# Two products over 64 contraction rows in plain float32, in pairs on the halves of the array, in an attention and mixture-of-experts kernel

## The reference, cut to what matters

```
spikes_enc = sigmoid(inputs_embeds @ W_enc + b_enc)          # 128 -> 256
cont = flat @ W_s2c + b_s2c                                  # 256 -> M = 64
probs = softmax(cont @ Wr + br)                              # 64 -> 8 experts
topk_w, topk_idx = top_k(probs, 2)                           # gates of the two best experts
h = relu(einsum('tm,emh->eth', cont, W1) + b1)               # 64 -> 128 for each of 8 experts
y = einsum('eth,ehm->etm', h, W2) + b2                       # 128 -> 64 for each expert
expert_out = einsum('etm,te->tm', y, gate)
spikes_moe = sigmoid(expert_out @ W_c2s + b_c2s)             # 64 -> 256
decoded = spikes_moe @ W_dec + b_dec                         # 256 -> 128
return layernorm(decoded, ln_g, ln_b)
```

## Time and profile before

| what | value |
|---|---|
| time, median of 3 runs | 162.12 us (161.94 to 162.26) |
| profiled execution, first to last instruction (its span; its own time is not listed apart from the runs) | 160.3 us |
| PE matmul busy, share of the span | 138.7 us, 87% |
| DVE busy | 130.0 us, 81% |
| ACT busy | 66.8 us, 42% |
| POOL busy | 29.9 us, 19% |
| granted PE clock | full until the last slices, then half of it |
| shares of the chain of waits that ended last | DVE 55%, PE 23%, issue 9% |

### The profile page before, as it was taken

One profiled execution on the slowest core, in us unless ns is written; L12 is line 12 of the kernel. 1 busy time (PEld: TensorE's weight loads), 2 busy tenths in 40 slices (PEclk: granted clock), 3 DMA queues, 4 the chain that ended last, 5 costly groups with the idle time before them and its releaser, 6 DMA issues.

```text
span 160.3 us, 2496 instructions
## 1 busy us (share of the span) xinstructions
PE 138.7 (87%) x820; PEld 104.4 (65%) x828; DVE 130.0 (81%) x504; ACT 66.8 (42%) x128; POOL 29.9 (19%) x55
## 2 busy tenths in 40 slices
PE   7697999589999989999999799999998889994810
PEld 2254686356589775768897757687994477983700
DVE  1686379999979996699999962897999759979883
ACT  3114662182961317467811246397203566003200
POOL 1452243102013100122211100204310002200131
PEclk9999999999999999999999999999999999999555
DMA  3499300000000000000010000000000010000101
GB/s 97 114 203 222 105 4 2 0 0 0 0 4 0 0 2 0 2 4 0 0 65 4 2 0 0 0 0 4 0 0 0 2 70 0 0 0 0 65 0 65
DMA packets 5597, 4.16 MB, mean 26 GB/s; under 512 B 1987, under 2 KB 4562, under 8 KB 5586
## 3 DMA queue, kind: packets, MB, share of 16 engines
q1 hardware_dynamic: 5586, 4.02, 9.3%
HBM read 2.97 MB, written 1.05 MB: 25 GB/s over the span
## 4 chain that ended last, share of the span: by engine, by line
DVE 55%; PE 23%; issue 9%; POOL 3%; SPq 2%; DMA 2%; ACT 2%; POOLq 1%; DVEq 0%
DVE stats L887 10%; DVE gated L1012 6%; DVE mean_var L890 4%; DVE moe L1022 4%; PE ps_f L718 4%; POOL rstd L352 3%; DVE neg_max L928 3%; DVE attn L903 3%; PE ps_f L638 3%; DVE hn L903 3%; PE ps_f L630 2%; PE ps_s L586 2%; DMA x_in<-in_L_attn_x 2%; DVE x_mid L945 2%; DVE z L1061 2%
## 5 line engine op out<-in xcount | busy, mean ns | idle before, releaser
L352 POOL TENSOR_TENSOR rstd<-var_eps,minus_half 128x2 f32<-128x2 f32 (+1 forms) x32 | 26.1, 815 | 122.9 <-DVE var_eps L896 104.1
L688 PEld LDWEIGHTS ps_f<-w,hidden 128*128 128x128 f32 x256 | 31.0, 192 | 1.8 <-issue 1.3
L688 PE MATMUL ps_f<-w,hidden 128*128 128x64 f32 x256 | 30.3, 272 | 0.5
L443 ACT ACTIVATE hidden<-ps_f,bias_cols 128x512 f32<-128x512 f32 x28 | 18.0, 689 | 9.2 <-PE ps_f L669 9.2
L1022 DVE TENSOR_REDUCE moe<-gated 128x64 f32<-128x512 f32 x16 | 16.6, 1035 | 0.1
L586 PE MATMUL ps_s<-kT,qT 128*128 128x512 f32 x32 | 16.3, 602 | 0.2 <-DVE kT L1092 0.2
L404 ACT ACTIVATE probs<-ps_s,neg_max 128x512 f32<-128x512 f32 x16 | 11.0, 685 | 8.3 <-DVE neg_max L928 8.3
L668 PE MATMUL ps_f<-cont_parts,w_hi 128*128 128x512 f32 x28 | 13.8, 493 | 0.3 <-DVE products L962 0.3
L928 DVE TENSOR_REDUCE neg_max<-ps_s 128x1 f32<-128x512 f32 x16 | 10.8, 685 | 2.9 <-PE ps_s L586 2.8
L409 ACT ACTIVATE probsT<-ps_t 128x512 f32<-128x512 f32 x16 | 9.6, 598 | 7.0 <-PE ps_t L596 7.0
L669 PE MATMUL ps_f<-cont_parts,w_lo 128*128 128x512 f32 x28 | 11.1, 395 | 0.0
(11 more groups left out here) (188 smaller groups left out, 250.8 us busy)
## 6 DMA issues: line engine op xcount, KB each, us to landing
x_in<-in_L_attn_x SPq DMA_DIRECT2D x4, 256.0 KB, 3.8
out<-x_out SPq DMA_DIRECT2D x3, 256.0 KB, 2.0
...
```

The lines of the kernel that those rows point to most:

```text
L352: nc.gpsimd.tensor_tensor(rstd[part], var_eps[part], minus_half[:, t0:t1], ALU.pow).then_inc(g_rstd[n], 1)
L443: nc.scalar.activation(hidden[:, e], hidden_bank(b, e)[:, :], ACT.Relu, bias=bias_cols[:, R_B1 + e:R_B1 + e + 1]).then_inc(a_h, 1)
L688: mm = nc.tensor.matmul(y[:, e * M:(e + 1) * M], hidden[:, e, t * P:(t + 1) * P], w2[:, e], start=False, stop=(e == E - 1))
```

## The change

The operands stay whole and plain float32. `cont` and `moeT` hold the same values in rows 0 to 63 and in rows 64 to 127 (ACT writes them as before, since the weights ahead of them stand twice), and a matmul takes 64 rows of both operands. Of a pair, the one with even number takes rows 0 to 63 and the odd one rows 64 to 127. The splits on DVE, and the waits for them, are gone: PE waits for ACT's `a_hi` and `a_mhi`. The order of PE's stream changes so that hidden units come in pairs. The orders of ACT, POOL and SP stay; DVE's only loses rows.

```
-    def hidden_units(b, e):
-        if e == 0:
-            pe.wait_ge(v_cont, b + 1)
-            if b == 0:
-                pe.wait_ge(v_w1, 2)
-        if e == 1 and 1 <= b < B - 1:
-            pe.wait_ge(v_z1, T * b)
-        if e == 2 and b < B - 1:
-            pe.wait_ge(v_prod, b + 1)
-        if e >= 3:
-            pe.wait_ge(a_h, E * b + e - 2)
-        bank = hidden_bank(b, e)
-        nc.tensor.matmul(bank[:, :], w1_hi[:, e], cont_parts[:, b % 2], start=True, stop=False)
-        nc.tensor.matmul(bank[:, :], w1_lo[:, e], cont_parts[:, b % 2], start=False,
-                         stop=True).then_inc(pe_h, 1)
+    def hidden_pair(b, e):
+        if e == 0:
+            pe.wait_ge(a_hi, b + 1)
+            if b == 0:
+                pe.wait_ge(d_w1, 32)
+            elif b < B - 1:
+                pe.wait_ge(v_z1, T * b)
+        for row in range(2):
+            if e + row == 2 and b < B - 1:
+                pe.wait_ge(v_logit, b + 1)
+            if e + row >= 3:
+                pe.wait_ge(a_h, E * b + e + row - 2)
+            half = slice(row * M, (row + 1) * M)
+            nc.tensor.matmul(hidden_bank(b, e + row)[:, :], w1[half, e + row], cont[half, b % 2],
+                             start=True, stop=True).then_inc(pe_h, 1)
...
-        mm = nc.tensor.matmul(logit_bank(b)[:, 2 * t * E:2 * (t + 1) * E],
-                              cont_parts[:, b % 2, t * P:(t + 1) * P],
-                              w_r[:, :, :].rearrange("p a e -> p (a e)"), start=True, stop=True)
+        mm = nc.tensor.matmul(logit_bank(b)[:, t * E:(t + 1) * E],
+                              cont[0:M, b % 2, t * P:(t + 1) * P], w_r[0:M, :], start=True, stop=True)
...
-    nc.tensor.matmul(slot(F_C2S[c])[:, :], w_c2s_hi[:, c * P:(c + 1) * P], moe_parts[:, b % 2],
-                     start=True, stop=False)
-    nc.tensor.matmul(slot(F_C2S[c])[:, :], w_c2s_lo[:, c * P:(c + 1) * P], moe_parts[:, b % 2],
-                     start=False, stop=True).then_inc(pe_c2s, 1)
+    for c in range(HC):
+        half = slice(c * M, (c + 1) * M)
+        nc.tensor.matmul(slot(F_C2S[c])[:, :], w_c2s[half, c * P:(c + 1) * P], moeT[half, b % 2],
+                         start=True, stop=True).then_inc(pe_c2s, 1)
...
         if more:
-            hidden_units(b, 0)
+            hidden_pair(b, 0)
         if first:
             turn_probs(n, 0)
             scores(n, 2)
-        if more:
-            hidden_units(b, 1)
-            hidden_units(b, 2)
+        hidden_pair(b, 2)
         if first:
             attend(n, 0)
             turn_probs(n, 1)
-        hidden_units(b, 3)
-        hidden_units(b, 4)
+            scores(n, 3)
+        hidden_pair(b, 4)
         if first:
-            scores(n, 3)
             attend(n, 1)
             turn_probs(n, 2)
-        hidden_units(b, 5)
-        hidden_units(b, 6)
-        if more:
             attend(n, 2)
             turn_probs(n, 3)
-        hidden_units(b, 7)
+        if b == 0:
+            attend(n, 2)
+            turn_probs(n, 3)
+        hidden_pair(b, 6)
...
             route(n)
-            for e in range(3):
-                hidden_units(n, e)
+            hidden_pair(n, 0)
             decode(b)
```

More of the change, by code:

```diff
@@ L116, in attention_moe_block @@
         spikes = sb("spikes", [P, 2, HC, S])
-        cont_parts = sb("cont_parts", [P, 2, S], F32R)
-        products = sb("products", [P, 2, T, E])
+        cont = sb("cont", [P, 2, S])
         logits = sb("logits", [P, 2, T, E])
@@ L132, in attention_moe_block @@
         moe = sb("moe", [P, 2, T, 2, M])
-        moe_parts = sb("moe_parts", [P, 2, S], F32R)
+        moeT = sb("moeT", [P, 2, S])
         spikes2 = sb("spikes2", [P, 2, HC, S])
@@ L315, in _ @@
             for half in range(2):
-                sp.dma_start(w1_raw[half * M:(half + 1) * M], W1.rearrange("e m h -> m e h")).then_inc(d_w1, 16)
+                sp.dma_start(w1[half * M:(half + 1) * M], W1.rearrange("e m h -> m e h")).then_inc(d_w1, 16)
             sp.dma_start(w_enc[:, :], W_enc).then_inc(d_enc, 16)
             for half in range(2):
-                sp.dma_start(w_r_raw[half * M:(half + 1) * M], Wr).then_inc(d_router, 16)
+                sp.dma_start(w_r[half * M:(half + 1) * M], Wr).then_inc(d_router, 16)
             sp.dma_start(br_all[:, :], br.partition_broadcast(P)).then_inc(d_router, 16)
@@ L325, in _ @@
             for half in range(2):
-                sp.dma_start(w_c2s_raw[half * M:(half + 1) * M], W_c2s).then_inc(d_c2s, 16)
+                sp.dma_start(w_c2s[half * M:(half + 1) * M], W_c2s).then_inc(d_c2s, 16)
             sp.dma_start(x_in[:, 2], x_dram[2]).then_inc(d_x[2], 16)
@@ L426, in cont_out @@
                     act.wait_ge(v_bcont, 1)
-                nc.scalar.activation(cont_parts[:, b % 2], slot(F_CONT)[:, :], ACT.Identity,
+                nc.scalar.activation(cont[:, b % 2], slot(F_CONT)[:, :], ACT.Identity,
                                      bias=b_cont[:, :]).then_inc(a_hi, 1)
@@ L432, in moe_out @@
                 act.wait_ge(pe_moeT, b + 1)
-                nc.scalar.activation(moe_parts[:, b % 2], slot(F_MT)[:, :], ACT.Identity).then_inc(a_mhi, 1)
+                nc.scalar.activation(moeT[:, b % 2], slot(F_MT)[:, :], ACT.Identity).then_inc(a_mhi, 1)
             def second_exp(b):
@@ L697, in turn_moe, with to_spikes @@
                 mm.then_inc(pe_moeT, 1)
-            def to_spikes(b, c):
-                pe.wait_ge(v_mparts, b + 1)
+            def to_spikes(b):
+                pe.wait_ge(a_mhi, b + 1)
                 if b + 1 < B:
@@ L728, in turn_last_moe, with last_to_spikes @@
                 mm.then_inc(pe_moeT, 1)
-            def last_to_spikes(c, h):
+            def last_to_spikes(h):
                 t0, t1 = LAST[h]
                 part = slice(t0 * P, t1 * P)
-                pe.wait_ge(v_mparts, B + h)
-                for weights, start in ((w_c2s_hi, True), (w_c2s_lo, False)):
-                    mm = nc.tensor.matmul(last_c2s[h][c][:, part], weights[:, c * P:(c + 1) * P],
-                                          moe_parts[:, (B - 1) % 2, part], start=start, stop=not start)
-                mm.then_inc(pe_c2s, 1)
+                pe.wait_ge(a_mhi, B + h)
+                for c in range(HC):
+                    half = slice(c * M, (c + 1) * M)
+                    nc.tensor.matmul(last_c2s[h][c][:, part], w_c2s[half, c * P:(c + 1) * P],
+                                     moeT[half, (B - 1) % 2, part], start=True, stop=True).then_inc(pe_c2s, 1)
             def decode_last(h):
@@ L857, in _ @@
                     to_cont(n)
-                for c in range(HC):
-                    to_spikes(b, c)
+                to_spikes(b)
                 if more2:
@@ L871, in _ @@
             expert_out(B - 1, T - 1)
-            for c in range(HC):
-                last_to_spikes(c, 0)
+            last_to_spikes(0)
             turn_last_moe(1)
             decode_last(0)
-            for c in range(HC):
-                last_to_spikes(c, 1)
+            last_to_spikes(1)
             decode_last(1)
@@ L961, in router_top @@
                 dve.wait_ge(pe_logit, b + 1)
-                nc.vector.tensor_reduce(products[:, i], logit_bank(b)[:, 0:2 * T * E].rearrange(
-                    "p (t a e) -> p t e a", t=T, a=2), AX_X, ALU.add).then_inc(v_prod, 1)
-                dve.wait_ge(v_prod, b + 1)
-                nc.vector.tensor_tensor(logits[:, i], products[:, i], br_all[:, :].unsqueeze(1).to_broadcast([P, T, E]),
+                dve.wait_ge(d_router, 48)
+                nc.vector.tensor_tensor(logits[:, i], logit_bank(b)[:, 0:T * E].rearrange("p (t e) -> p t e", t=T),
+                                        br_all[:, :].unsqueeze(1).to_broadcast([P, T, E]),
                                         ALU.add).then_inc(v_logit, 1)
@@ L1211, in _ @@
                     z_unit(b - 1, 0)
-                if more:
-                    split_moe(b)
                 if more and not more2:
@@ L1221, in _ @@
                     x_norm(m + 1)
-                if more:
-                    split_cont(n)
             z_unit(B - 2, 0)
-            split_last_moe(1)
             z_add(B - 2, 0)
```

58 lines of the change are left out of this document (7 added, 51 removed).

## The result

| what | before | with the change |
|---|---|---|
| time, median | 162.19 us (161.94 to 162.49, 4 runs) | 172.61 us (171.72 to 173.71, 4 runs) |
| ratio | | 1.064, 95% interval 1.0576 to 1.0705 |
| span of the profiled execution | 160.3 us | 169.7 us |
| PE matmul busy | 138.7 us, 87% | 148.7 us, 88% |
| DVE busy | 130.0 us, 81% | 120.8 us, 71% |

The change makes the kernel 6.4% slower, by 10.4 us; the forecast was 170.8 us and the range 165.3 to 177.8. The four runs lie on two levels, 171.7 at a mean granted clock of 0.960 and 173.5 to 173.7 at 0.943; the profiled one is on the lower, and its span is 9.4 above that of before, where 8.7 was forecast.

The account below looks back on a forecast made before the run. Neither DVE nor PE alone was taken to bound the kernel; the chain changes sides. 0.2 + 2.8 + 3.1 + 0.5 + 2.55 - 0.65 + 0.2 = +8.7 on 162.1 gave 170.8 us, range 165.3 to 177.8.

Parts of the forecast that it names:

- pass 0: First pass, order kept but for the pairing: fourth pair +0.3 at expert_out, slack leaves +0.2 (from -0.8 to +1.5).
- `to_spikes`, twice: Product with W_c2s in passes 0 and 1, 1.28 where it took 1.04: +0.5 (from -0.4 to +1.3).
- pass 1: First pair waits for v_z1 with turn_probs and scores queued behind; ACT's copy uncovered; DVE's gates later by +2.8.
- pass 2: Begins like pass 1, with attend(3, 3) ahead of expert_out and turn 3's copy ahead of relu 6: +3.1.
- pass 2 to 3: Unit 2 stands behind decode(2), so second_exp, gates and dec_stats wait: statistics at 135.7, not 133.14, +2.55.
- the end: Last sequence: -0.65 left of DVE's saved 1.40, +0.2 for last_to_spikes(1) in float32 at the low clock.
- price of a pair: Two hidden units on two halves take 1.28 by in-order starts (bounds 0.85 and 1.70), 0.96 before.
- side by side: Rival: a pair's records interleave on the two halves, pair 0.85, queue waits remain: +3.9, time 166.0; chance 0.20.
- switching between half and whole rows: On PE, taken as costing nothing; upper bound 0.20 at each of some 20 switches, +4.
- drains: Rival: changing tiling mode drains the engine, +8.7 and up to 4 more, 174.8 at the most; chance 0.12.
- relief of DVE: Last sequence: the 1.40 us for ACT's copy and split before DVE's gates goes; some -0.65 is left.
- rival of the earlier clock: Rival: PE idles some 2.6 us ahead of turn_last_moe(0), clock falls, expert_out(3) takes 1.7 more: 172.5; chance 0.05.

Follow-up runs that it names:

- experiment 6: The changed kernel with all hidden units and both W_c2s blocks on rows 0 to 63, so pairs cannot overlap: 183.15 us in one run, without an interval.
- Experiments 6 and 7: The changed kernel with all units and W_c2s blocks on one half (183.15 us, one run), or on all 128 rows with doubled sums halved (177.25 us, ratio 1.092).
- experiment 1: The changed kernel with units put back singly in their old places and waits, operands still float32 on half the rows: 168.30 us, ratio 1.037.
- experiment 8: The kernel before, with split float32r operands and DVE's splits, but PE's order from the change: 167.70 us, ratio 1.032.
- experiment 2: The changed kernel with unit 2 of the last sequence put ahead of decode(2) again: 168.95 us, ratio 1.041.

## Why the prediction was right, and where it was not

**Direction and size hold** and most terms with them, the size in part by luck, as said below. From the table, with forecast and measured value:

| term | forecast | measured |
|---|---|---|
| pass 0 | +0.2 | +0.98 (A) |
| `to_spikes`, twice | +0.5 | +0.71 (B, D) |
| pass 1 | +2.8 | +2.70 (C) |
| pass 2 | +3.1 | +2.82 (E) |
| pass 2 to 3 | +2.55 | +2.30 (F) |
| the end | -0.45 | -0.14 (G) |

**The price of a pair was right for a wrong reason.** I took 1.28 from in-order starts: the odd unit begins with the even one's second record. The rows at 139.51 contradict that, and so does experiment 6: side by side, a pair costs 0.85. The step that failed is the one on switching between half and whole rows: "I take nothing, since neighbours of different kinds in rows 4 follow without a gap". Those neighbours differ in type and width, but all stand on 128 rows; none of them switches. Experiments 6 and 7 measure the switch at 0.39, and 0.85 + 0.39 = 1.24 happens to be near 1.28. That is luck, and through it so is the nearness of 170.8. Two rivals that I had kept apart, side by side and drains, were true at once: +3.9 and at most +4, where their sum of 7.9 is also near the result. The Trainium skill has both: TensorEngine Tiling (Array Packing), Key Properties, says that a change of tiling mode drains the engine, and the 0.39 of experiments 6 and 7, with loads that no longer run ahead, is in keeping with it. The Trainium skill, TensorE: Matmul & The Clock Gate, Measured speedup vs the span model, gives a pack about the duration of one matmul, and 1.05 for one unit, 1.06 for two (experiment 1) agree.

**Pass 0** was mis-sized by 0.8. I let only the fourth pair count (+0.3) and took the rest as hidden behind `relu`. PE in pass 0, two rows of before, then three of the change:

```profile
44.48 1.05 PE L609 MATMUL ps_o<-v,probsT 128*128 128x128 f32 x8
45.73 0.48 PE L668 MATMUL ps_f<-cont_parts,w_hi 128*128 128x512 f32 x1
```

```profile
44.69 1.16 PE L597 MATMUL ps_o<-v,probsT 128*128 128x128 f32 x8
46.21 1.13 PE L655 MATMUL ps_f<-cont,w 64*128 64x512 f32 x4
47.50 2.11 PE L674 MATMUL ps_f<-w,hidden 128*128 128x64 f32 x16
```

The first three pairs follow each other and make one stay, and they wait for ACT's `relu` rather than for PE's work, so `attend(1, 2)` starts only 0.21 later. The sum of prices begins behind it: 0.27 more up to the fourth pair, 0.51 more for that pair, which replaces one unit. `expert_out` thus starts 0.99 later (47.50 for 46.51). It also takes 0.22 longer (2.11 for 1.89), since unit 6 now stands behind `turn_probs(1, 3)` too, ACT does its `relu`, the copy and `relu` 7 in a row, and the last product waits for `relu` 7. The prediction's "keeps its order but for the pairing" had overlooked that. Of the 1.21 the slack of 0.21 is taken off. The old order has +1.50, and the new order without the price 0: here the price is what costs.

**Pass 1 and 2** came out by the queue as worked out. The first gates of pass 1 start 14.26 behind the first pair (71.53 to 85.79; forecast 14.3), with PE's price for a pair at 1.27 and not 1.28. PE idles 0.61 for `v_z1`, and `attend(n, 2)` waits 0.69 for ACT's copy, which no two units cover any longer. By experiments 1 and 8 the order alone gives 1.10 and 1.36 of these stretches and the price alone 2.09 and 2.50. The two overlap, by the stay that the new order saves.

**Pass 2 to 3** is the order alone: +2.04 without the price (experiment 8), +0.07 without the order (experiment 1), and one unit moved ahead takes it away (experiment 2). Of the 2.65 that the sum has at `e_sum` (134.6 for 131.95), 2.30 came; the 2.55 forecast for the statistics behind it are 2.13.

**The end.** The relief of DVE was forecast at -0.65 and its counterpart at +0.2. Behind `e_sum` the change gains 0.14. The relief is there: the third gates come 1.68 sooner behind `e_sum` (9.53 for 11.21). Of it 0.25 is left at the fourth. PE idles there too, 1.42 us and not the 2.6 of the rival, ahead of the first transposes, and then meets the lower clock:

```profile
151.15 0.44 PE L712 MATMUL ps_s<-ident,moe 128*128 128x128 f32 x2 [1.42 <-DVE moe L976]
...
151.64 2.45 PE L674 MATMUL ps_f<-w,hidden 128*128 128x64 f32 x16
...
154.12 0.69 DVE L984 TENSOR_TENSOR gated<-ps_f,gate 128x512 f32<-128x512 f32 x1 [1.35 <-PE ps_f L674]
```

`expert_out(3)` takes 2.45 in its record where it took 1.89, and DVE waits 1.35. The granted clock is 0.78 in the window from 150 to 155 us and 0.54 from 155 to 160, that is mostly the lower level, 1.2 GHz. So the rival of the earlier clock came in part, some 0.56 of its 1.7 in the profiled run. Whether the rest of it makes the upper of the two levels of time (173.5) is open: their mean clock is lower, 0.943, but none of those runs has a trace.
